# Moving the fetch and the split of the first four routed experts' weights from beats 3 to 15 to beats 10 to 19 of the shared part

## What is computed

```python
h = relu(einsum('td,ndf->ntf', flat, shared_w1) + shared_b1[:, None, :])      # 2 shared experts
out = flat + einsum('ntf,nfd->td', h, shared_w2) + shared_b2.sum(0)
scores = sigmoid(flat @ centroids.T) + bias
vals, idx = top_k(scores, 4)                                                   # 4 of 16 routed experts
gating = scatter(vals, idx); gating = gating / clip(gating.sum(-1), 1e-8)
for w1, b1, w2, b2, g in routed experts: rout += (relu(flat @ w1 + b1) @ w2 + b2) * g
```

## Time and profile before

| quantity | value |
| --- | --- |
| median of three runs | 1152.22 us (1148.06 to 1154.04) |
| profiled execution: own time, span | 1140.37 us, 1138.5 us |
| busy PE / DVE / ACT / POOL | 86% / 61% / 59% / 45% |
| mean granted TensorE clock | 0.955 |
| DMA, mean | 150 GB/s |
| chain that ended last: PE, DVE, ACT, DMA, issue | 58%, 13%, 9%, 8%, 8% |

### The profile page before, as it was taken

One profiled execution on the slowest core, in us unless ns is written; L12 is line 12 of the kernel. 1 busy time (PEld: TensorE's weight loads), 2 busy tenths in 40 slices (PEclk: granted clock), 3 DMA queues, 4 the chain that ended last, 5 costly groups with the idle time before them and its releaser, 6 DMA issues.

```text
span 1138.5 us, 27350 instructions
## 1 busy us (share of the span) xinstructions
PE 977.9 (86%) x9516; PEld 562.2 (49%) x9516; DVE 697.1 (61%) x1661; ACT 672.3 (59%) x1099; POOL 512.8 (45%) x442
## 2 busy tenths in 40 slices
PE   5889989987899999999999999955999989888830
PEld 2555556555667677777777677732222222111120
DVE  8676665568888544344344332217587788867686
ACT  4655644544444255565566544436778888899930
POOL 0232332146777456666566555522222555343423
PEclk9999999998999999999999999987899999999965
DMA  6534231369985188888888777884688787686211
GB/s 240 186 125 139 92 127 56 139 180 174 197 199 112 54 276 171 177 179 206 188 201 174 160 129 120 155 135 132 139 154 165 180 177 159 150 175 138 58 38 66
DMA packets 184819, 171.35 MB, mean 150 GB/s; under 512 B 137444, under 2 KB 140068, under 8 KB 183780
## 3 DMA queue, kind: packets, MB, share of 16 engines
q1 hardware_dynamic: 157650, 112.33, 39.4%
q0 software_dynamic: 25888, 56.43, 24.6%
q10 hardware_dynamic: 1154, 0.87, 0.2%
HBM read 80.87 MB, written 65.20 MB: 128 GB/s over the span
## 4 chain that ended last, share of the span: by engine, by line
PE 58%; DVE 13%; ACT 9%; DMA 8%; issue 8%; POOL 2%; ACTq 0%; SPq 0%; POOLq 0%; DVEq 0%
PE ps_shpY L1523 11%; PE ps_shpH L1534 11%; PE ps_shpH L402 6%; ACT sb_atp L2110 6%; PE ps_shpY L1469 4%; PE ps_shpY L845 4%; PE ps_atpO L1869 4%; PE ps_shpH L835 4%; PE ps_shpH L1459 4%; PE ps_atpO L1893 3%; DMA x2a<-sb_roy,sb_roentry 2%; DMA sb_shxT<-sb_shxhl 2%; PE ps_atpS L1857 2%; DMA sb_roxg<-xn,sb_roentry 1%; PE ps_atpO L1876 1%
## 5 line engine op out<-in xcount | busy, mean ns | idle before, releaser
L2110 ACT ACTIVATE sb_atp<-ps_atpS 128x1024 f32<-128x1024 f32 x256 | 242.2, 1036 | 32.5 <-PE ps_atpS L1857 32.5
L1534 PEld LDWEIGHTS ps_shpH<-sb_roxT,sb_rowt 128*128 (+1 forms) x2844 | 167.2, 106 | 18.8 <-issue 0.4
L1534 PE MATMUL ps_shpH<-sb_roxT,sb_rowt 128*128 128x128 f16 (+1 forms) x2844 | 171.8, 219 | 0.1
L1523 PE MATMUL ps_shpY<-sb_rowt,sb_rohhl 128*128 (+1 forms) x711 | 166.4, 379 | 5.8 <-DVE sb_rohhl L1397 5.7
L1869 PE MATMUL ps_atpO<-sb_atp,sb_atv 128*17 128x512 f32 x1024 | 135.6, 601 | 29.1 <-ACT sb_atp L2110 27.9
L1235 ACT ACTIVATE sb_roh<-ps_shpH,sb_rob 128x128 f32<-128x128 f32 (+1 forms) x237 | 69.1, 362 | 75.5 <-PE ps_shpH L1534 67.9
L1132 POOL DMA_INDIRECT sb_roxg<-xn,sb_roentry x79 | 86.5, 1095 | 50.9 <-issue 27.0
L1523 PEld LDWEIGHTS ps_shpY<-sb_rowt,sb_rohhl 128*128 128x128 f16 (+1 forms) x711 | 66.5, 98 | 72.2 <-issue 7.1
L1224 ACT ACTIVATE sb_roy<-ps_shpY,sb_roentry 128x512 f32<-128x512 f32 x79 | 54.1, 685 | 72.2 <-PE ps_shpY L1523 42.4
L1144 POOL DMA_INDIRECT x2a<-sb_roy,sb_roentry x40 | 68.1, 1703 | 58.1 <-ACT sb_roy L1224 47.9
L1120 POOL DMA_INDIRECT list<-sb_shentry,sb_shposb x64 | 73.2, 1144 | 40.5 <-DVE sb_shposb L1307 25.3
(11 more groups left out here) (353 smaller groups left out, 1742.8 us busy)
## 6 DMA issues: line engine op xcount, KB each, us to landing
sb_rowt<-rw SPq DMA_DIRECT2D x15, 768.0 KB, 8.4
sb_rowt<-rw SPq DMA_DIRECT2D x15, 704.0 KB, 5.6
kst<-sb_kykp SPq DMA_DIRECT2D x16, 512.0 KB, 4.5
qst<-sb_quqp SPq DMA_DIRECT2D x12, 512.0 KB, 3.9
vst<-sb_kyvt SPq DMA_DIRECT2D x16, 272.0 KB
sb_atv<-vst SPq DMA_DIRECT2D x32, 136.0 KB, 3.4
sb_stage<-ctxT SPq DMA_DIRECT2D x4, 1024.0 KB, 6.4
sb_shxin<-x SPq DMA_DIRECT2D x16, 256.0 KB, 7.2
```

What stands on the lines that cost most here:

```text
L1523: last = e.matmul(pY[it.p][:, :], hhl[it.p][0:n, x, k * P:(k + 1) * P], weight(value, 2 * W1 + w + k * D, n, D), start=j == 0, stop=j == l ...
L1534: last = e.matmul(rpH[it.p][0:n, f * P:(f + 1) * P], weight(ex["up"], w + k * FF + f * P, P, n), rxT[it.p][:, x + k, :], start=j % (3 * KD ...
L2110: S.done(e.activation(pr[n % 6][:, :], pS[n % 3][:, :], ACT.Exp, scale=HD ** -0.5 / SA ** 2), "atexp")
```

## The change

One line, which sets where the four early experts are split, and with the lag of -2 where they are fetched.

```diff
-        early_beat = {5 + 3 * k: k for k in range(EARLY)}
+        early_beat = {12 + 2 * k: k for k in range(EARLY)}
```

## The result

| | before | after |
| --- | --- | --- |
| median of the comparison's runs | 1148.61 us (22 runs, 1142.6 to 1156.86) | 1143.78 us (22 runs, 1139.15 to 1151.79) |
| ratio, 95% interval | 1 | 0.9954 (0.9939 to 0.9968) |
| profiled execution: own time, span | 1140.37, 1138.5 us | 1143.92, 1142.1 us |
| busy PE / DVE / ACT / POOL | 86 / 61 / 59 / 45% | 86 / 61 / 59 / 45% |

The change is faster by 0.46%, some 5 us. The forecast was 1149.4 us and 2.8 us faster. Of these 5.6 us, 3.6 us is the base: the median of before was 1152.2 us over three runs and is 1148.6 us over 22. The other 2.0 us is gain: the medians lie 4.8 us apart, not 2.8 us. Two later comparisons of the same two kernels gave 0.9981 (0.9956 to 1.0006) and 0.9961 (0.9928 to 0.9995).

What follows compares the result with a forecast made beforehand. PE was taken to bound the kernel from 314.3 to 388.5 us, with transpose waits before; 6.8 - 1.0 - 1.3 - 1.7 = 2.8 us faster, from 1152.2 to 1149.4 us, range 1145.0 to 1158.0 us.

Steps and rivals of the forecast that it cites:

- Won, 6.8 us at tiles 7 and 8: PE before 315 us: waits at `route`(7) and `route`(8) and slow matmuls go, 4.37 + 1.18 + 1.28 us; bounds 0 and 6.8.
- The 4.37 us and 1.18 us at `route`(7): PE's wait for transpose 7, 4.37 us, and slower `down`(4) matmuls behind it, 1.18 us; both taken as won.
- rival 2: `route`(7): its stall stays for a reason neither fetch nor split; 2.7 us slower, 1154.9 us; chance 0.20.
- I cost their removal at nothing: Beats 3 to 9: removing fetches of experts 0 and 1 and halves on beats 5 and 6 changes time by nothing.
- Lost, 1.0 us behind a fetch: Beats 10 and 11: expert 0's fetch delays transpose 9; 1.0 us lost, taken between 0 and 3.7 us.
- rival 1: Transposes 9, 11, 13, 15: a fetch delays the transpose behind it; 6.6 us slower, 1158.8 us; chance 0.15.
- The row that I called nearer: Transpose 11, issued 7.1 us after expert 3's fetch without a wait at `route`(11): 0 us, the lower case for transpose 9.
- Lost, 1.3 us by DVE's drift: Beats 12 to 16: split halves delay transpose issue 0.77 us a beat; 1.3 us lost, bounds 0 and 6.8.
- meeting POOL at another moment: DVE's split beats: without lock contention with POOL the drift and its 1.3 us vanish, making the sum 4.1 us.
- the deadline sum: Transposes on SP: each must land 12.3 us after PE began the beat of issue, with 5.4 us taken for landing.
- Lost, 1.7 us in the tail: Beat 19: the half between table and `hidden`(14) delays `numbers` and first gather; 1.7 us lost, bounds 0 and 1.8.
- rival 3: Split beats and tail: the costs hide; 6.8 us faster, 1145.4 us; chance 0.15.

Runs made afterwards that it cites:

- e5: The change unchanged, timed against before: ratio 0.9981 (0.9956 to 1.0006); profile 72.5 us from `route`(0) to `route`(8), 61.3 us on to `route`(15).
- e2: The change unchanged, profile alone: 1145.5 us; 65.7 us from `route`(0) to `route`(8), 67.4 us on to `route`(15).
- e17: The change unchanged, profile alone: 66.6 us from `route`(0) to `route`(8), 65.6 us on to `route`(15).
- e9: The change with each fetch issued in two pieces one beat apart (704 KB, then 768 KB): ratio to before 0.9971 (0.9945 to 0.9997).
- e8: Before unchanged, profile alone: 67.5 us from `route`(0) to `route`(8), 57.9 us on to `route`(15).
- e11: Before unchanged, profile alone: 70.3 us from `route`(0) to `route`(8), 58.1 us on to `route`(15).
- e18: The change unchanged, profile alone: 69.2 us from `route`(0) to `route`(8), 68.3 us on to `route`(15).
- e3: The change with its fetches put back to SP beats 3, 6, 9, 12, only the split halves late: ratio to before 1.0026 (1.0 to 1.0051).
- e6: The change with DVE's last split half moved ahead of `place`(15) and the table: ratio to before 0.9993 (0.9969 to 1.0018).
- e4: The change two beats earlier, fetches on SP beats 8, 10, 12, 14, halves on 10 to 17: ratio to before 1.0039 (1.0009 to 1.0069).
- e12: Before unchanged, timed against itself: ratio 1.0007 (0.9977 to 1.0036); its profile has 7.2 us of idle gaps inside `up`.
- e13: The change unchanged, timed against before: ratio 0.9961 (0.9928 to 0.9995); its profile has 11.0 us of idle gaps inside `up`.
- e10: Before with the early experts' fetches cut to 16 columns per matrix, split halves kept at full width: ratio to before 0.9959 (0.9938 to 0.998).
- e14: The change with fetches cut in two pieces and DVE's last half ahead of `place`(15): ratio to before 0.9941 (0.9911 to 0.9971).
- e1: Before unchanged, profile alone: 1136.1 us; 71.4 us from `route`(0) to `route`(8), 58.0 us on to `route`(15).
- e15: Before unchanged, profile alone: 75.1 us from `route`(0) to `route`(8), 60.1 us on to `route`(15).

## Why the prediction was right and wrong

**The base: 3.6 us too high.** The forecast subtracts its gain from 1152.2 us, the median of three runs; 22 runs have 1148.6 us. From that base the forecast would have been 1145.8 us, 2.0 us above the measured time.

**Won, 6.8 us at tiles 7 and 8: half of it in the traces, and mostly at other tiles.** In the executions without gaps the head shrank from 71.86 us (six of before) to 68.53 us (four of the change), 3.3 us in place of 6.8. The 4.37 us and 1.18 us at `route`(7) were one execution's: the wait is 2.1 us on average before and 2.4 us in the change. That is rival 2's mechanism, a transpose late for a reason that is neither fetch nor half, and I gave it 0.20. What the change did win there is `route`(8), 1.9 to 0.4 us, and `route`(5) and `route`(6), 1.4 to 0.2 us. So the step that failed is "I cost their removal at nothing", for the fetches of experts 0 and 1, together with the choice of tile 7 for the gain. It holds for `route`(3), whose transpose is late with or without them, but not for tiles 5 and 6, which the one trace that I read does not show waiting.

The clock's part follows the wait, as the prediction had it. Windows of the 18 matmuls of `down`(4), first in after, where `route`(7) waited for nothing:

```profile
303.67:307.55 3.88, 3.88 (x24) 1.74 (x21) 3.42 (x17) 3.16 (x9) 2.03 (x3) 1.00 1.02 278
```

and then in e5, behind its 4.94 us:

```profile
303.44:309.31 5.87, 5.87 (x25) 2.24 (x21) 4.12 (x18) 3.19 (x9) 3.72 (x4) 0.66 1.05 185
```

The gaps of 1.81 and 1.19 us inside `up` just before the first of these left the granted clock at 1.00; others in the same trace did not, as the last section shows. I had put 1.18 us of slower matmuls behind the wait at `route`(7), and none behind those that the 1.0 us below stands for.

**Lost, 1.0 us behind a fetch: under-sized.** I priced transpose 9 alone. Transposes 13 and 15 wait too, and the middle grew in the profiled executions from 58.5 us to 65.7 us. The waits at tiles 9, 13 and 15 are 5.8 us of the change's 65.7 us, and the 2.0 us that are left over the 57.9 us are matmuls at a lower clock behind them. That is rival 1's mechanism, at three of the four places that it named; its sign, a wait of over 3 us before `route`(9), is in e2 and e17. The Trainium skill (DMA: Bandwidth & Descriptors, Queues, rings and completion order) has it that each DMA engine consumes the descriptors of one queue in ring order; e2's transpose 9, 12.6 us behind 1472 KB of weights, and e9's 1.24 us behind one piece, agree with it. e5's transpose 7 has no weights ahead of it in the queue, only stores and a row load, whose landings the trace does not give, so it neither bears the rule out nor speaks against it. The row that I called nearer, transpose 11 some 7.1 us after a fetch, was not luck but a special case: where the traces of before and of the change give its landing, it took 3.5 to 4.4 us (e2, e8, e11, e18), and it was late in none of them. Why tile 11 is spared, and 9, 13 and 15 are not, is open.

**Lost, 1.3 us by DVE's drift: the drift came, a wait by it alone did not.** e3 has the same halves on the same beats. Its transposes 11 to 14 go out 5.8, 6.5, 7.2 and 7.9 us into PE's beats 13 to 16 (transpose 14 at 365.74 us, by its SP timeline), which is the drift as forecast; so meeting POOL at another moment did not take it away. That leaves transpose 14 some 4.4 us to land, and PE's beats stay at 8.27 us, so it landed within those 4.4 us, not the 5.4 us that I took. The drift is not free in the change: e2's transpose 15 went out 6.3 us into its beat, by the deadline sum, where before it was 5.1 us, and that is an estimated 1.2 us of its wait of 3.38 us. The deadline model was right in form; its landing times were not constants. In time, e3 is 3.0 us slower than before; the tail explains 1.6 us, and the other 1.4 us is inside its interval.

**Lost, 1.7 us in the tail: right.** 1.3 us in after, 1.6 us in e2, e5, e17 and e18, against bounds of 0 and 1.8; e6 and e4, without a half at that place, have none of it.

**The time.** The timed runs say 4.5 us faster, plus or minus 1.4; the forecast said 2.8. The sign was right, and the forecast gain lies just outside that interval. As a ratio the change stayed within 0.5%; but the line drawn for "faster by over 0.5%", 1146.4 us, stood on the base that was too high, and the measured 1143.8 us is below it. It is nearest to rival 3's 1145.4 us. That rival, that the costs hide, is not what the traces show: the drift made no wait alone, but the tail's cost is in every profiled execution of the change, and waits behind the fetches are in all but one. That the time came out near rival 3 is the lower base plus a gain between the two forecasts, and no merit of the mechanism.

**What stays open.** The profiled executions without gaps have the change longer in all: head -3.3 us, middle +7.1 us, the rest up to the routed part +2.9 us (1.6 us in the tail, the other 1.3 us before `numbers`, where a late `route`(15) is followed by 18.0 us in place of 16.3 us), 6.7 us in sum (161.6 against 154.9 us). The timed runs, three comparisons, have it shorter. Behind the first routed transposes the spans spread from 738 to 747 us (738 to 745 us in before and in the change alike), so the sum of the shared part is not the whole, but a mean over six and four executions should not be off by 11 us for that. In the one pair with gaps from the same chip (e12, e13) the shared part is 1.6 us shorter with the change, which is the sign of the timed runs. Single executions also lie oddly against the timed medians: of the five of before that came in a round with enough timed runs, four took 8.2, 7.6, 3.7 and 1.0 us less than before's median and one 1.4 us more, while in the eleven runs with timed runs of their own the profiled execution took 3.0 us more than that median on average (from 1.5 us less to 7.4 us more). That a profiled execution treats DMA queues in another way than a timed one would explain the contradiction; nothing here tests that. So what is shown of the cause is what the timed ratios show (e3 and e10 above all): the gain comes from moving the transfers away from beats 3 to 12, not from moving the halves. Which of the waits in the traces it goes back to is argued, not shown; the waits at tiles 5, 6 and 8 are the candidates, since they come with the early fetches.

## What to carry to other kernels

Before pricing the removal of a wait on a DMA, take several profiled executions of the kernel before: here the wait that carried the sum (4.37 us) was 0 to 4.94 us from one to the next, with and without the transfer that I blamed. To see what a transfer costs, shrink it and keep its consumers' work, and separately keep it and move the consumers; these two timed runs (e10 and e3) settled what no reading of waits could. In a queue that also carries work with a deadline, a bulk fetch was better placed behind the stretch where other stores share the queue (the change against e4); cutting it in pieces made the waits of one trace smaller, and its worth in time is not shown. And take the base from as many runs as the forecast is fine: three runs were 3.6 us off here, more than the gain that was forecast.

## What the runs showed of the hardware

- **Gaps inside straight runs of matmuls.** PE stood still up to 2.4 us at a time, 5.9 to 11.0 us in an execution, inside `up`, with no releaser. The same executions have more of them elsewhere: 0.5 to 1.6 us in L1869 and 0.4 to 1.1 us in L1974 (the cross attention; L1872 and L1977 in e14), and 0.3 to 2.5 us in L303, where the sixteen others have none. So they belong to the whole execution and not to the shared part. (Idle times without a releaser are nothing rare in themselves: L845, in the first block, has 12.9 to 14.1 us of them in every execution.) In the timeline of PE of e12, which is before unchanged:

```profile
329.89 0.22 PE L1459 MATMUL ps_shpH<-sb_shxT,sb_shw 128*96 128x128 f16 x1 [0.71 <-issue]
330.63 0.22 PE L1459 MATMUL ps_shpH<-sb_shxT,sb_shw 128*96 128x128 f16 x1 [0.53 <-issue]
332.09 3.93 PE L1459 MATMUL ps_shpH<-sb_shxT,sb_shw 128*96 128x128 f16 x39 [1.24 <-issue]
```

  They came in after and in the three executions e12, e13 and e14, which ran on chip 14 in one round, and were absent or 0.4 us in all others. It is not the chip by itself: e1 to e4 ran on chip 14 too, in an earlier round, and had none. Their cause is open.
- **The granted clock fell behind some gaps and not behind others.** In after, 1.81 and 1.19 us just ahead of `route`(7) left it at 1.00 (the window of `down`(4) above). Behind 0.81, 0.50 and 0.46 us near 328 us it was 0.70 from 329 to 331 us and 0.50 from 331 to 333 us, and a pair of matmuls took 1.01 us, where it takes 0.59 us at the full clock:

```profile
328.75 3.36 PE L1459 MATMUL ps_shpH<-sb_shxT,sb_shw 128*96 128x128 f16 x38 [0.46 <-issue]
...
332.33 1.01 PE L1469 MATMUL ps_shpY<-sb_shw,sb_shhh 128*128 128x512 f16 x2
```

- **The landing time of one 128 x 1024 transpose scatters.** It took 3.0 us (e17, transpose 6) to 12.7 us (e15, transpose 8) where the traces give it. In e5 it took 11.9 us with no weights in flight, while the DMA moved 145 and 167 GB/s, by its windows, less than the 278 GB/s of the window of after shown above. The DMA engines were not idle: their busy share was 1.40 and 0.83, against 1.02 in that window of after, so in the first of the two they were busier for fewer bytes:

```profile
294.00:298.00 4.00, 4.00 (x73) 3.95 (x71) 1.35 (x2) 1.58 (x2) 2.72 (x3) 1.00 1.40 145
298.00:302.00 4.00, 0.10 (x2) 0.00 (x0) 3.81 (x6) 0.00 (x0) 1.65 (x2) 0.83 0.83 167
```

- **The same kernel differs from one round of timing to the next by more than the change does.** The median of before was 1137.6 us in one round (chip 6) and 1152.9 us in another (chip 14), 1.3% apart, three times the effect. On chip 14 alone it was 1143.7 us in an earlier round, so most of that is not a matter of the chip; only ratios within a round mean something at this size.
